# The last two steps of a ternary rounding go from DVE to PE and ACT, and the opening's order is written anew

## The reference, cut to what matters

```python
w = w_fp32.astype(jnp.bfloat16)
w_g = w.reshape(-1, g)
scale = jnp.clip(jnp.mean(jnp.abs(w_g), axis=-1, keepdims=True), 1e-08, None)
q = jnp.clip(jnp.round(w_g / scale), -1, 1)
w_hat = (q * scale).reshape(w.shape)
return w + jax.lax.stop_gradient(w_hat - w)
```

## Time and profile before

| | |
|---|---|
| median of 3 runs | 848.24 us |
| the profiled execution, its own time | 850.22 us |
| its span | 848.5 us |
| busy: PE, DVE, ACT, POOL | 795.6, 766.5, 682.1, 690.7 us |
| mean granted clock of PE | 0.993 |

### The profile page before, as it was taken

The page is one execution under the profiler, slowest core; times in us unless marked ns, Lnnn a source line. Parts: engine busy times, 40 slices in busy tenths (PEclk is TensorE's granted clock), DMA queues, the critical chain, the costliest instruction groups (busy, mean ns, idle before and its releaser), DMA issues.

```text
span 848.5 us, 23834 instructions
## 1 busy us (share of the span) xinstructions
PE 795.6 (94%) x9723; PEld 470.6 (55%) x9723; DVE 766.5 (90%) x1503; ACT 682.1 (80%) x1331; POOL 690.7 (81%) x689
## 2 busy tenths in 40 slices
PE   5798999889999999999999999999999999999996
PEld 2344545555556666555666565556665565555553
DVE  5999999989999999999999999999999888879763
ACT  2475658768888989988888888989899888779864
POOL 4898478979989999999999999999999886465741
PEclk9899999999999999999999999999999999999999
DMA  8100211112243333333432323433433233335334
GB/s 258 58 8 8 70 33 41 34 46 43 60 71 65 72 69 77 77 71 71 77 77 62 72 61 69 76 72 70 70 78 70 64 71 48 71 74 82 77 68 94
DMA packets 125117, 58.00 MB, mean 68 GB/s; under 512 B 93072, under 2 KB 124048, under 8 KB 125008
## 3 DMA queue, kind: packets, MB, share of 16 engines
q1 hardware_dynamic: 125008, 56.49, 32.0%
HBM read 13.98 MB, written 4.19 MB: 21 GB/s over the span
## 4 chain that ended last, share of the span: by engine, by line
PE 70%; DVE 14%; ACT 6%; SPq 4%; issue 2%; DMA 2%; POOL 2%; POOLq 0%; DVEq 0%; ACTq 0%
PE ps L840 9%; PE ps L647 6%; PE ps L902 5%; PE ps L916 5%; PE ps L888 5%; PE ps L809 4%; PE ps L715 4%; PE ps L774 4%; SPq L307 3%; PE ps L697 3%; PE ps L685 3%; DVE rowmax L3884 3%; PE ps L657 3%; PE ps L754 2%; DMA k_rows<-qk_lo 2%
## 5 line engine op out<-in xcount | busy, mean ns | idle before, releaser
L3884 DVE TENSOR_REDUCE rowmax<-ps 128x4 f32<-128x768 f32 x256 | 243.1, 950 | 9.5 <-PE ps L774 8.6
L2203 ACT ACTIVATE prob<-ps 128x768 f32<-128x768 f32 x256 | 207.2, 809 | 28.8 <-PE ps L809 28.3
L3276 POOL TENSOR_TENSOR hsum<-hsum,minus_half 128x32 f32<-128x32 f32 x32 | 175.9, 5496 | 14.7 <-DVE hsum L3809 14.7
L3301 POOL TENSOR_SCALAR_AFFINE_SELECT prob<-prob 128x512 f32<-128x512 f32 (+1 forms) x128 | 112.4, 878 | 28.0 <-ACT prob L2203 27.6
L3303 POOL TENSOR_SCALAR_AFFINE_SELECT prob<-prob 128x1024 f32<-128x1024 f32 (+1 forms) x128 | 113.3, 885 | 0.0
L840 PE MATMUL ps<-prob,v_pad 128*32 128x192 f32 x2048 | 96.5, 329 | 0.0
L774 PE MATMUL ps<-k_rows,q_rows 31*128 31x192 f16 x1024 | 86.3, 246 | 7.6 <-DVE rowmax L3884 3.6
L809 PE MATMUL ps<-q_rows,k_rows 32*128 32x192 f16 x1024 | 86.3, 246 | 1.5 <-ACT prob L2203 1.2
L840 PEld LDWEIGHTS ps<-prob,v_pad 128*32 128x32 f32 x2048 | 60.0, 109 | 29.3 <-issue 16.8
L888 PE MATMUL ps<-wgu,xsplitT 128*128 128x512 bf16 x256 | 65.7, 381 | 4.9 <-ACT v_own L2112 4.3
L902 PE MATMUL ps<-wgu,xsplitT 128*128 128x512 bf16 x256 | 66.5, 383 | 3.6 <-DVE heads L3910 2.2
(11 more groups left out here) (162 smaller groups left out, 2035.4 us busy)
## 6 DMA issues: line engine op xcount, KB each, us to landing
v_swap<-v_own SPq DMA_DIRECT2D x64, 68.0 KB, 2.1
xin<-in_x SPq DMA_DIRECT2D x32, 128.0 KB, 2.5
q_rows<-qk_hi SPq DMA_DIRECT2D x64, 64.0 KB, 2.0
k_rows<-qk_hi SPq DMA_DIRECT2D x64, 64.0 KB, 2.1
enc<-in_ctx SPq DMA_DIRECT2D x32, 128.0 KB, 2.3
out<-yout SPq DMA_DIRECT2D x32, 128.0 KB, 2.0
prob<-in_w_guT SPq DMA_DIRECT2D x4, 512.0 KB, 7.6
q_rows<-qk_lo SPq DMA_DIRECT2D x32, 64.0 KB, 2.0
```

Source lines behind the costliest of these rows:

```text
L2203: copy(prob[:, 2 * c:2 * c + 2, :, :].rearrange("p u a b -> p u (a b)"), ps[:, STB:STB + 2, 0:2 * QW], ACT.Exp, scale=float(XD) ** -0.5).t ...
L3276: g.tensor_tensor(hsum[:, t.two, 1, :], hsum[:, t.two, 0, :], minus_half[:, :], ALU.pow).then_inc(S["head_pow3"], 1)
L3301: g.affine_select(out=lead, in_=lead, compare_op=ALU.is_ge, fill=0.0, base=BAND - 64 * kb, pattern=[[0, 8], [1, cut]], channel_multiplier=-1)
L3884: v.tensor_reduce(of_head[:, hq:hq + 2, 2 * row_of(ng):2 * row_of(ng) + 2], ps[:, MXB:MXB + 2, 0:2 * QW].rearrange("p j (a b) -> p j a b", ...
```

## The change

1. DVE keeps parts 1 to 3 of `quantise`, and part 3 ends with the product, signalled on `s_whole`. Part 4 is gone, and so is the subtraction.
2. PE makes difference and sum, for each half (512 columns) of a chunk: `diff_weights(n, half)` writes identity times product and negated identity times weight, added up, to the bank `OTB`; `add_weights(n, half)` does the same for rounded difference and weight.
3. ACT rounds the difference from PSUM to `wtmp[:, n % 2, 1]` (`round_diff`) and writes the sum from PSUM to `wgu` or `wproj` (`store_weights`), which raises `s_wq`, now by 12 in all. It also makes the negated identity `minusb` once. `do_val(tile[0], 0)` waits for all twelve stores, since it writes to the same bank.
4. The opening of all five queues is in another order. The stages in it are the same, apart from the rounding's. The matmuls of `keep_warm` are 78 in place of 153, nearly all of them in bank 0, 5 or 7. `cut_bias` stands ahead of `do_variance(tile[1])`. The loop of steps is not touched.

The core of the diff (for PE, ACT, SP and DVE the beginning of the new order; it goes on in this way up to the loop):

```diff
--- before.py
+++ after.py
...
+        minusb = sb("minusb", [128, 128], BF16)
...
-            do_xload(tile[5])
             sp.wait_ge(S["v"], tile[0].at(1, 1))
             do_vswap(tile[0])
             sp.wait_ge(S["v"], tile[1].at(1, 1))
             do_vswap(tile[1])
+            do_xload(tile[5])
+            do_enc(tile[0])
             sp.wait_ge(S["v"], tile[2].at(1, 1))
             do_vswap(tile[2])
             sp.wait_ge(S["y1"], tile[0].at(1, 1))
             do_xload(tile[6])
+            do_vswap(tile[3])
             sp.wait_ge(S["y1"], tile[1].at(1, 1))
             do_xload(tile[7])
...
+            def diff_weights(n, half):
+                cut = slice(512 * half, 512 * half + 512)
+                pe.wait_ge(s_whole, n + 1)
+                if n == 0 and half == 0:
+                    pe.wait_ge(s_fold, 3)
+                    pe.wait_ge(s_wround, 1)
+                else:
+                    pe.wait_ge(s_wq, 2 * n + half)
+                mm(ps[:, OTB, :], identb[:, :], wtmp[:, n % 2, 0, cut], start=True, stop=False)
+                mm(ps[:, OTB, :], minusb[:, :], wq16[:, n % 2, cut], start=False, stop=True).then_inc(s_wdiff, 1)
+
+            def add_weights(n, half):
+                cut = slice(512 * half, 512 * half + 512)
+                pe.wait_ge(s_wround, 2 * n + half + 2)
+                mm(ps[:, OTB, :], identb[:, :], wtmp[:, n % 2, 1, cut], start=True, stop=False)
+                mm(ps[:, OTB, :], identb[:, :], wq16[:, n % 2, cut], start=False, stop=True).then_inc(s_wadd, 1)
+
...
                 if t.base == 0 and n == 0:
+                    pe.wait_ge(s_wq, 2 * WCHUNKS)
                     pe.wait_ge(s_fold, 3)
...
             do_qk_ps(tile[0])
-            turn_bias()
-            carry_bias()
             pe.wait_ge(S["xn"], tile[1].at(1, 1))
             do_xnT_ps(tile[1])
+            turn_bias()
             pe.wait_ge(S["xnT"], tile[1].at(1, 1))
+            do_v_ps(tile[0])
+            carry_bias()
             pe.wait_ge(S["qk"], tile[0].at(1, 1))
             do_qk_ps(tile[1])
-            do_v_ps(tile[0])
-            keep_warm(1)
+            keep_warm(7, 0)
             sum_weights(0)
-            keep_warm(12)
+            pe.wait_ge(S["v"], tile[0].at(1, 1))
+            do_xnT_ps(tile[2])
+            keep_warm(1, 0)
+            pe.wait_ge(S["xnT"], tile[2].at(1, 1))
+            pe.wait_ge(S["qk"], tile[1].at(1, 1))
+            do_qk_ps(tile[2])
+            keep_warm(7, 0)
             sum_weights(1)
-            pe.wait_ge(S["v"], tile[0].at(1, 1))
+            keep_warm(3, 0)
+            diff_weights(0, 0)
+            keep_warm(3, 0)
+            add_weights(0, 0)
+            keep_warm(3, 0)
+            diff_weights(0, 1)
             do_v_ps(tile[1])
-            keep_warm(2)
-            pe.wait_ge(S["v"], tile[1].at(1, 1))
-            do_xnT_ps(tile[2])
-            keep_warm(2)
-            pe.wait_ge(S["xnT"], tile[2].at(1, 1))
-            do_qk_ps(tile[2])
-            keep_warm(9)
+            add_weights(0, 1)
             pe.wait_ge(S["qkn"], tile[0].at(1, 1))
             pe.wait_ge(S["qk"], tile[2].at(1, 1))
             do_qkT_ps(tile[0])
-            keep_warm(11)
+            keep_warm(5, 0)
+            diff_weights(1, 0)
+            keep_warm(3, 0)
             pe.wait_ge(S["qkT"], tile[0].at(1, 1))
             do_s_ps(tile[0])
-            keep_warm(8)
-            sum_weights(2)
...
-                    act.wait_ge(s_wq, n - 1)
+                    act.wait_ge(s_wq, 2 * (n - 1))
                 copy(wtmp[:, n % 2, 0, :], wraw[:, n, :], ACT.Abs)
                 copy(wtmp[:, n % 2, 1, :], wraw[:, n, :], ACT.Sign)
                 copy(wq16[:, n % 2, :], wraw[:, n, :], ACT.Copy).then_inc(s_wparts, 1)
+                if n == 0:
+                    act.wait_ge(s_const, 16 * CONSTS)
+                    copy(minusb[:, :], identb[:, :], ACT.Copy, scale=-1.0).then_inc(s_wround, 1)
+
+            def round_diff(n, half):
+                act.wait_ge(s_wdiff, 2 * n + half + 1)
+                copy(wtmp[:, n % 2, 1, 512 * half:512 * half + 512], ps[:, OTB, :], ACT.Copy).then_inc(s_wround, 1)
+
+            def store_weights(n, half):
+                act.wait_ge(s_wadd, 2 * n + half + 1)
+                if n < 4:
+                    at = HID * (n % 2) + 512 * half
+                    dst = wgu[:, n // 2, at:at + 512]
+                else:
+                    at = 4 * (n - 4) + 2 * half
+                    dst = wproj[:, at:at + 2, :].rearrange("p b d -> p (b d)")
+                copy(dst, ps[:, OTB, :], ACT.Copy).then_inc(s_wq, 1)
+
             def do_x_eps(t):
                 if t.base == 0:
...
             do_x_eps(tile[1])
+            act.wait_ge(S["x_stats"], tile[2].at(1, 1))
+            do_x_eps(tile[2])
             act.wait_ge(S["xn_nb"], tile[1].at(1, 1))
             do_xn(tile[1])
             act.wait_ge(S["xnT_ps"], tile[1].at(1, 1))
             do_xnT(tile[1])
-            weight_parts(0)
-            do_x_eps(tile[2])
             act.wait_ge(S["xn_nb"], tile[2].at(1, 1))
             do_xn(tile[2])
+            weight_parts(0)
+            act.wait_ge(S["v_ps"], tile[0].at(1, 1))
+            do_v(tile[0])
+            act.wait_ge(S["xnT_ps"], tile[2].at(1, 1))
+            do_xnT(tile[2])
+            act.wait_ge(S["centred"], tile[0].at(1, 1))
             do_squared(tile[0])
             weight_parts(1)
-            act.wait_ge(S["v_ps"], tile[0].at(1, 1))
-            do_v(tile[0])
+            round_diff(0, 0)
+            store_weights(0, 0)
+            round_diff(0, 1)
+            act.wait_ge(S["x_stats"], tile[3].at(1, 1))
+            do_x_eps(tile[3])
+            do_squared(tile[1])
             act.wait_ge(S["v_ps"], tile[1].at(1, 1))
             do_v(tile[1])
-            act.wait_ge(S["centred"], tile[1].at(1, 1))
-            do_squared(tile[1])
-            act.wait_ge(S["xnT_ps"], tile[2].at(1, 1))
-            do_xnT(tile[2])
-            act.wait_ge(S["x_stats"], tile[3].at(1, 1))
-            do_x_eps(tile[3])
+            store_weights(0, 1)
             act.wait_ge(S["qkT_ps"], tile[0].at(1, 1))
             do_qkT(tile[0])
+            round_diff(1, 0)
             weight_parts(2)
+            store_weights(1, 0)
             act.wait_ge(S["xn_nb"], tile[3].at(1, 1))
             do_xn(tile[3])
             act.wait_ge(S["s_sub"], tile[0].at(1, 1))
...
             def quantise(n, part):
-                w16 = wq16[:, n % 2, :]
                 size, sign = wtmp[:, n % 2, 0, :], wtmp[:, n % 2, 1, :]
                 if part == 1:
                     dve.wait_ge(s_wsum, n + 1)
+                    if n:
+                        dve.wait_ge(s_whole, n)
                     v.tensor_scalar(wscale[:, :].rearrange("p (a b) -> p a b", a=2), ps[:, STB:STB + 2, :],
                                     1.0 / GROUP, 1e-8, ALU.mult, ALU.max).then_inc(s_wscale, 1)
                 if part == 2:
@@ -3753,14 +3831,8 @@
                     link(v.scalar_tensor_tensor(size, wscale[:, :], 257.0 / 512.0, size, ALU.mult, ALU.is_lt))
                     link(v.tensor_tensor(size, size, sign, ALU.mult))
                 if part == 3:
-                    link(v.tensor_tensor(size, size, wscale[:, :], ALU.mult))
-                    link(v.tensor_tensor(size, size, w16, ALU.subtract))
-                if part == 4:
-                    if n < 4:
-                        done = v.tensor_tensor(wgu[:, n // 2, HID * (n % 2):HID * (n % 2) + HID], w16, size, ALU.add)
-                    else:
-                        done = v.tensor_tensor(wproj[:, 4 * (n - 4):4 * (n - 4) + 4, :].rearrange("p b d -> p (b d)"), w16, size, ALU.add)
-                    done.then_inc(s_wq, 1)
+                    v.tensor_tensor(size, size, wscale[:, :], ALU.mult).then_inc(s_whole, 1)
+
             def do_x_stats(t):
                 chain = Chain("x_stats_c", t, 4)
                 chain(v.bn_stats(stat[:, 0, 0:6], xin[:, t.x_buf, :]))
...
-            fold_bias()
             dve.wait_ge(S["x_pow"], tile[1].at(1, 1))
             do_xn_nb(tile[1])
-            hold_bias()
+            fold_bias()
             dve.wait_ge(S["qk_ps"], tile[0].at(1, 1))
             do_qk(tile[0])
+            dve.wait_ge(S["x_pow"], tile[2].at(1, 1))
+            do_xn_nb(tile[2])
+            hold_bias()
+            add_bias()
             scale_gains()
-            add_bias()
-            cut_bias()
             dve.wait_ge(S["qk_ps"], tile[1].at(1, 1))
             do_qk(tile[1])
             dve.wait_ge(S["rotated"], tile[0].at(1, 1))
             do_centred(tile[0])
-            dve.wait_ge(S["x_pow"], tile[2].at(1, 1))
-            do_xn_nb(tile[2])
             quantise(0, 1)
-            quantise(0, 2)
             dve.wait_ge(S["squared"], tile[0].at(1, 1))
             do_variance(tile[0])
+            quantise(0, 2)
+            dve.wait_ge(S["qk_ps"], tile[2].at(1, 1))
+            do_qk(tile[2])
+            quantise(0, 3)
```

(89 more changed lines are left out.)

612 lines of the change are left out of this document (301 added, 311 removed).

## The result

The changed kernel takes 841.98 us (median of 16 runs, 839.41 to 847.94); the kernel before took 848.72 on the same chip (16 runs, 847.88 to 851.33). The ratio is 0.9927 (0.9915 to 0.9938): about 6.2 us less. I had forecast 840.4.

A forecast was written before the change was run, and what follows sets the result against it. DVE was taken to bound the opening, whose gain passes one for one through an unedited loop: -11.4 (DVE) + 4.8 (handoffs) - 1.2 (fillers) = -7.8 us, 848.24 to 840.4. Range 838 to 842.3, chance 0.40.

The forecast's parts named there:

- What goes from DVE: Opening, ahead of the loop: 12 subtractions and additions leave DVE, so the loop begins 11.4 us sooner if DVE stays dense.
- The handoffs: Opening: 24 new ACT evictions and their waits for PE make DVE 4.8 us later, 0.2 each; ends 0 and 14.4.
- forecast some 12 us in all: DVE's idle time from 26 us to the 32nd `rowmax`: some 12 us in place of 7.8.
- the rule of a sixth: Opening: a sixth of ACT's 29 us for new evictions and waits shows as lateness on DVE, 4.8 us.
- my slower rival: Opening: ACT's queue becomes the bound, each of 24 evictions costs 0.65 us on the path, 851.2 us; chance 0.11.
- Fillers: PE's opening: 75 fillers fewer against 48 new matmuls, 27 fewer net at 0.043 us each, a gain of 1.2 us.
- a fall or two of 1.3 us: PE's opening: fewer fillers may bring one or two more clock falls, 1.3 us each, inside the range.
- `cut_bias`: Opening's head: moved later on the same queue, POOL's first power some 4 us sooner; 1.5 worse to 4 better, taken as 0.
- Entry to the loop: 161.8 to 195 us: DVE's 5.3 us idle after a `qk_lo` transfer could shrink by up to 4.3; taken as 0.
- The sum: Whole kernel: -11.4 + 4.8 - 1.2 = -7.8 us, from a median of 848.24 to 840.4 us.

## Why the prediction was right, and where it was not

**What goes from DVE: 11.4 us.** Right in its kind and near in size. 12.1 us went from DVE's opening, and the path had no slack for them: put back idle, 11.55 us cost 13.7; with PE's matmuls equal, 10.8 cost 12.8. But in either pair the slower kernel also lost 6.6 us more of clock. At after's 0.81 us for each us lost (see the last paragraph but one of this section) that would be 5.3 us, which leaves 8.4 and 7.5 us for DVE's work itself. So what is shown is the price of DVE's work together with the clock that falls with it; the two are not separated. The idle operations also stand ahead of the product, so PE gets each product later than it would with the work behind it.

**The handoffs: 4.8 us, 0.2 each.** The size of the change in DVE's idle time was near (forecast some 12 us in all, measured 14.0), but the reason was not. Leaving every handoff out made the kernel 2.4 us slower, with 3.7 us more of clock lost, some 3.0 us at the same 0.81: nothing is left over for the 24 handoffs, give or take 2 us. Doubling the evictions cost 2.0 us for 11.2 of ACT's time, the rule of a sixth; for the 14.4 us of new evictions that is 2.5 us, not 4.8. What came back as idle time is the new order's: of the 6.2 us, 5.5 are `rowmax` waiting longer for PE (6.6 in place of 1.1), and it waits as long in the new order without handoffs and with DVE's work put back. The prediction had no term for that. That my 4.8 stood where 6.2 were measured is luck.

In the old order, as I placed them, the same 24 handoffs go with 26.7 - 7.84 = 18.9 us more of DVE's idle time, 0.8 each if all of it is theirs, and with 853.98 us, where my slower rival had 851.2. No kernel has that order and fillers without the handoffs, so their share is not shown. The prediction took the handoffs as a property of the move and said nothing of what the move would cost without the new order.

**Fillers: -1.2 us.** The price was wrong. I had read from the chain what fillers cost on the path, 0.043 us each, and set what they protect at a fall or two of 1.3 us. Leaving out 79 of before's costs 6.7 us, 0.085 each, where that price gives a gain of 3.4; leaving out after's 78 costs 7.0, 0.09 each. The 48 matmuls of the rounding are fillers too (they gained 4.3 us where nothing depended on them), which I counted as load and not as cover, so the change has net 27 fewer. For these last 27 even the sign is open: at 0.085 each they would be a loss of 2.3 us, but putting 22 into after, almost the number of before, made it 2.1 us slower, not faster. Nor did after keep before's falls: the one at 28 to 32 us is gone, with the clock at 1.00 in all of 24 to 104 us, and another stands at 108 to 116.

**`cut_bias`: 0.** POOL's first power starts 5 us sooner, as expected (4). DVE is as busy in the first stretch as before (32.74 and 32.59), and its second `amax` starts 2.0 us sooner (57.76 for 59.80); the fall that is gone and the operations removed from DVE ahead of it can give that as well. I ran nothing on this step alone.

**Entry to the loop: 0, up to -4.3.** -1.5 us in the profiled pair from the 32nd `rowmax` to the tenth `amax`, 56.26 and 54.79 us. It was before's profile that was long: the kernel with half of before's fillers, whose order is before's, took 54.29, and the move in the old order 54.11. So it is no gain of the change, and my 0 stands.

**The sum.** In the profiled pair the opening ends 6.0 us sooner (12.1 us less of DVE's work, 6.2 more of its idle time), the entry gives 1.5 and the loop 2.5; together 10.0, of which only the 6.0 are shown to be the change's. The ratio of the medians says 6.2. The profiled execution of before lies 1.5 us above its median and that of after 1.7 below. Part of this is the clock: the profiled execution of after lost 3.4 us of it, the mean of its 16 timed ones 6.3. Over these 16 the span follows the lost clock with 0.81 us for each (correlation 0.92); over the executions of other kernels here the slope was anything from 0 to 0.8, so what I work out with 0.81 is an estimate at its upper end. Of DVE's 14.0 us of idle time 2.9 lie in the 8 us at the low clock and 3.7 in the 12 us from 128 on at full clock. Why PE serves `rowmax` later in the new order I did not take apart.

**The parts do not add.** The move alone, as I placed it, costs 6.4 us, the order alone with PE's matmuls kept 9.0, together they gain 6.2. My forecast was of the whole, and only the whole came near it: for either half it would have been wrong by more than its range. How much of the 6.4 is my placing and how much the old order stays open: I made one placing only.

## What to carry to other kernels

Work on the engine that paces a stretch can cost its whole time even when that engine shows 14 us idle; test it by putting the time back as work that does nothing, and look at the clock of the other engine before you call all of it the work's price. Before you put new idle time down to the new handoffs, leave the handoffs out: here it stayed, and went with the order. A handoff back to back was 1.3 us of ACT's queue each; what it costs the kernel depends on what stands around it, so a move and the order around it have to be judged together. Count matmuls that move to PE as cover for its clock as well as load, and find the number of fillers from both sides: 0, 78, 85 and 100 gave ratios of 1.0009, 0.9927, 0.9933 and 0.9952. Compare one profile with one profile only stage by stage: a loop that no kernel changed differed by 4.3 us between profiles.

## What the runs showed of the hardware

PE's granted clock fell although PE was far from idle. In after it was busy 3.39 and 3.00 of 4 us in the two stretches up to the fall to 0.50. PE's timeline there (the 64 small matmuls of `do_o_ps` lie between the first two of these rows; the last three ran at the lower level for most or all of their time):

```profile
104.93 0.20 PE L739 MATMUL ps<-v_own,probT_a 64*64 64x17 f32 x1 [0.41 <-DVE prob_a L3899]
...
105.84 0.21 PE L739 MATMUL ps<-v_own,probT_a 64*64 64x17 f32 x1
...
107.57 1.23 PE L778 MATMUL ps<-x,wx_qk 64*128 64x256 f32 x4 [0.36 <-ACT negmax L2249]
108.58 0.96 PE L782 MATMUL ps<-wx_v,x 64*128 64x64 f32 x8
...
109.90 2.08 PE L681 MATMUL ps<-wqkv,xnT 128*128 128x256 f32 x4
```

The last group took 1.03 us at the higher level, and the one at 107.57 took 0.70 at 130.33. In before one fall followed 5.37 us without a matmul, and I had taken that as what a fall needs. With 22 fillers more, most of them around such stretches, the clock was 0.998 to 1.000 in all seven executions. Executions of one kernel differ in where the falls come, and with it in time: after's 16 run from 839.4 to 847.9 us, so one profile does not show what the clock costs a kernel.
